# The last attention of four layers recut: scores made turned, their maximum as one more row, and two heads' values side by side

## The reference

```python
def _L3_xattn_ref(x, latents, ...):          # x: context, latents: layer-normed x
    xn = layer_norm(x, ln_media_w, ln_media_b)
    zn = layer_norm(latents, ln_lat_w, ln_lat_b)
    q = (zn @ Wq)                             # 8 heads of 64
    kv_in = jnp.concatenate([xn, zn], axis=1) # 64 + 1024 = 1088 keys
    k, v = kv_in @ Wk, kv_in @ Wv
    sim = jnp.einsum('bhqd,bhfd->bhqf', q * scale, k)   # scale = 1/8
    alphas = jax.nn.softmax(sim, axis=-1)
    out = jnp.einsum('bhqf,bhfd->bhqd', alphas, v)
    return out @ Wout

x = x + jnp.tanh(g_ffn[2]) * _L2_ffn_ref(_layernorm(x, axis=-1), ...)     # quantised
x = x + jnp.tanh(g_xattn[3]) * _L3_xattn_ref(ctx_1024, _layernorm(x, axis=-1), ...)
x = x + jnp.tanh(g_ffn[3]) * _L3_ffn_ref(_layernorm(x, axis=-1), ...)
```

## Time and profile before

| | us |
|---|---|
| median of 3 runs | 2302.47 |
| lowest and highest run | 2296.79, 2312.04 |
| the profiled execution | 2311.39 |
| span of the profiled core, first to last instruction | 2309.5 |
| TensorE busy | 1847.4 (80%) |
| VectorE busy | 1343.0 (58%) |
| ScalarE busy | 1051.7 (46%) |
| GpSimd busy | 570.2 (25%) |
| mean granted clock of TensorE | 0.879 |

### The profile page before, as it was taken

The page is one execution under the profiler, slowest core; times in us unless marked ns, Lnnn a source line. Parts: engine busy times, 40 slices in busy tenths (PEclk is TensorE's granted clock), DMA queues, the critical chain, the costliest instruction groups (busy, mean ns, idle before and its releaser), DMA issues.

```text
span 2309.5 us, 30543 instructions
## 1 busy us (share of the span) xinstructions
PE 1847.4 (80%) x10608; PEld 1326.6 (57%) x10608; DVE 1343.0 (58%) x2559; ACT 1051.7 (46%) x2069; POOL 570.2 (25%) x800
## 2 busy tenths in 40 slices
PE   6643999808975788884998687899999999986895
PEld 3243998805653322253554355688888888873553
DVE  4942444354758466651112688688888888843334
ACT  3112434203226777731221344687876787730340
POOL 2133000072347444432000455101001000105014
PEclk8756999959978699985999887899999999987997
DMA  9112222120000000042112100000000000022343
GB/s 368 45 62 74 105 89 109 36 75 1 1 18 1 1 1 1 1 174 92 32 37 76 37 1 1 1 1 1 1 1 1 1 1 1 1 101 72 99 135 91
DMA packets 60099, 112.53 MB, mean 49 GB/s; under 512 B 7829, under 2 KB 51288, under 8 KB 57520
## 3 DMA queue, kind: packets, MB, share of 16 engines
q1 hardware_dynamic: 52272, 90.02, 11.0%
q0 software_dynamic: 7680, 20.57, 2.8%
HBM read 71.12 MB, written 39.80 MB: 48 GB/s over the span
## 4 chain that ended last, share of the span: by engine, by line
PE 62%; DVE 14%; POOL 8%; ACT 7%; issue 5%; DMA 2%; another core or an unknown queue 1%; SPq 0%; POOLq 0%; DVEq 0%; ACTq 0%
PE psum L203 53%; PE psum L2005 4%; POOL arena L1577 2%; POOL arena L781 2%; ACT arena L1376 2%; POOL xb L776 2%; PE psum L237 1%; DVE arena L518 1%; DVE arena L208 1%; DVE arena L218 1%; POOL arena L678 1%; DVE arena L1458 1%; ACT arena L2067 1%; DVE rounded L2089 1%
## 5 line engine op out<-in xcount | busy, mean ns | idle before, releaser
L203 PE MATMUL psum<-arena 128*128 128x256 f32 (+17 forms) x4423 | 1036.9, 448 | 184.7 <-DVE arena L1492 30.6
L203 PEld LDWEIGHTS psum<-arena 128*128 128x128 f32 (+5 forms) x4423 | 559.6, 177 | 577.7 <-issue 345.1
L203 PE MATMUL psum<-rounded 128*128 128x256 f32 (+5 forms) x3648 | 559.1, 308 | 20.0 <-DVE rounded L817 19.6
L203 PEld LDWEIGHTS psum<-rounded 128*128 128x128 f32 (+2 forms) x3648 | 493.9, 189 | 57.9 <-issue 17.7
L2089 DVE SCALAR_TENSOR_TENSOR rounded<-psum,rounded 128x512 fp32r<-128x512 f32 (+4 forms) x456 | 255.8, 586 | 92.8 <-ACT rounded L2075 43.6
L2075 ACT ACTIVATE rounded<-psum 128x512 fp32r<-128x512 f32 (+1 forms) x320 | 164.6, 553 | 35.8 <-PE psum L2009 18.7
L781 POOL DMA_INDIRECT arena<-yb,arena x80 | 78.0, 974 | 409.2 <-DMA yb<-arena 363.4
L1376 ACT ACTIVATE arena<-psum,arena 128x1024 f32<-128x1024 f32 (+1 forms) x192 | 156.5, 911 | 46.5 <-PE psum L203 46.4
L2115 DVE TENSOR_REDUCE arena<-psum 128x1 f32<-128x1024 f32 x128 | 155.4, 1214 | 1.0 <-PE psum L203 1.0
L2005 PE MATMUL psum<-arena 128*128 128x128 f32 x1024 | 141.3, 278 | 13.2 <-ACT arena L2070 9.3
L2067 ACT ACTIVATE arena<-psum,arena 128x1024 f32<-128x1024 f32 x128 | 143.7, 1123 | 1.7 <-DVE arena L2117 1.7
(11 more groups left out here) (251 smaller groups left out, 2071.3 us busy)
## 6 DMA issues: line engine op xcount, KB each, us to landing
arena<-in_w SPq DMA_DIRECT2D x8, 2048.0 KB, 7.6
yb<-arena SPq DMA_DIRECT2D x102, 128.0 KB
xb<-arena SPq DMA_DIRECT2D x5, 2048.0 KB, 17.3
arena<-xb SPq DMA_DIRECT2D x70, 128.0 KB, 2.2
arena<-in_w1u SPq DMA_DIRECT2D x4, 2048.0 KB, 14.8
arena<-xb SPq DMA_DIRECT2D x8, 512.0 KB
arena<-in_w1d SPq DMA_DIRECT2D x1, 4096.0 KB, 13.5
arena<-in_w3b SPq DMA_DIRECT2D x1, 4096.0 KB, 16.9
```

What stands on the lines that cost most here:

```text
L203: return e.matmul(o, l, r, start=start, stop=stop, skip_group_check=True)
```

## The change

The stage is cut into 16 blocks (G) of one pair of heads and 512 queries; `a` is the head of the pair, j one of nine key tiles (eight of 128 keys, one of the 64 of the context).

- Scores are made turned: keys in PSUM's partitions, 512 queries in its columns. So the exponentials come out as the value matmuls want them, and the transposes, their copies and low parts go. `K1`/`Q1` hold the high part of the head `a`'s k and q in one half of the rows and k's high part (a copy) against q's low part in the other; `K2`/`Q2` hold k's low part against q's high part, and, in rows that were free, ones against the negated maximum. Each score is the sum of two rounded matmuls.
- The maximum now is a rough one, from the high parts alone: an unturned score product of one pass (`pe_rough3`), a maximum on VectorE (`dve_rough3`, `dve_maxima3`), turned on TensorE (the "m" side step) and copied into `Q2` as one more row. It is made for block G + 1 while block G runs.
- Values: v and the exponentials stay unrounded float32. Two matmuls of 64 weight columns, one for each head, write the halves of bank 4's partitions (`pe_values3`).
- The sums over keys: GpSimd adds up the exponentials of the nine tiles (`pool_sum3`), a matmul with ones sums over partitions (the "s" side step), and VectorE takes the reciprocal in four parts and multiplies (`dve_divide3`). The result is already as the output projection ("o") wants it.
- Side steps (q, k, v, m, s, o) come at fixed steps j of a block (`side3`), all in PSUM bank 7 after the first ones.
- The first three side steps are moved into `pe_mid`, `act_mid` and `dve_mid` (rounds 18 to 22); the loads of the next stage's weights come earlier.

```diff
@@ dve_mid, pe_mid, act_mid
+                if 20 <= i < 23 and STAGES >= 7:
+                    dve_side3(e, FIRST3[i - 20])
...
+                if i == 18:
+                    e.wait_ge(s_w3, 16)
+                    e.wait_ge(s_xt, 52)
+                    e.wait_ge(s_scp, NT)
+                if 18 <= i < 21 and STAGES >= 7:
+                    pe_side3(e, FIRST3[i - 18])
...
+                if 18 <= i < 21 and STAGES >= 7:
+                    act_side3(e, FIRST3[i - 18])
@@ the order of the side steps
+        FIRST3 = [("k", 0, 0), ("k", 0, 1), ("q", 0, 0), ("k", 0, 2), ("v", 0, 0), ("v", 0, 1), ("v", 0, 2), ("q", 1, 0),
+                  ("m", 0, 0)]
+        FIRST_BANK3 = (0, 1, 2, 7, 0, 1, 4, 7, 7)
+        def side3(G, j):
+            n = G // 2
+            if j == 1 and G:
+                return ("s", G - 1, 0)
+            if j == 2 and G + 2 < 16:
+                return ("q", G + 2, 0)
+            if 3 <= j <= 5 and n + 1 < 8:
+                return ("v" if G % 2 else "k", n + 1, j - 3)
+            if 6 <= j <= 7 and G >= 7 and (G - 1) // 2 % 4 == 3:
+                return ("o", G - 1, j - 6)
+            if j == 8 and G + 1 < 16:
+                return ("m", G + 1, 0)
+            return None
@@ side steps
+        def pe_side3(e, s):
+            kind, a, c = s
+            bk, was = SIDE3_BANK[s], SIDE3_WAS[s]
+            if was is not None:
+                if was[0] == "o":
+                    e.wait_ge(s_x, 96 + tiles3(was[1], was[2])[1] + 1)
+                elif was[0] in "kq":
+                    e.wait_ge(s_lo3, SIDE3_LOW[was])
+                else:
+                    e.wait_ge(s_mo, SIDE3_KEPT[was])
...
+            if kind == "k":
+                n = 512 if c < 2 else 64
+                for k in range(2):
+                    m = mm(e, psum[:, bk, 0:n], x3_WK[:, k, 128 * p:128 * p + 128], src[:, k, :], k == 0, k == 1)
+            elif kind == "v":
+                for x in range(4 if c < 2 else 1):
+                    for k in range(2):
+                        m = mm(e, psum[0:rows, bk, 128 * x:128 * x + 128], src[:, k, rows * x:rows * x + rows],
+                               x3_WV[:, k, 128 * p:128 * p + 128], k == 0, k == 1)
+            elif kind == "q":
+                b, p, h = block3(a)
+                for k in range(2):
+                    m = mm(e, psum[:, bk, :], x3_WQ[:, k, 128 * p:128 * p + 128],
+                           XT[:, k, 1024 * b + 512 * h:1024 * b + 512 * h + 512], k == 0, k == 1)
+            elif kind == "m":
+                e.wait_ge(s_mx, 48 + a + 1)
+                for t in range(4):
+                    m = mm(e, psum[0:65, bk, 128 * t:128 * t + 128], x3_NM[:, t, :], ident, True, True)
+            elif kind == "s":
+                e.wait_ge(s_pa, 8 * a + 8)
+                for x in range(2):
+                    m = mm(e, psum[64 * x:64 * x + 64, bk, :], ones[:, 0:64], x3_AC[:, a % 2, x, :], True, True)
...
+        def act_side3(e, s):
...
+            if kind == "k":
+                for x in range(2):
+                    src = psum[high3(x), bk, 0:512 if c < 2 else 64]
+                    for r in (high3(x), high3(1 - x)):
+                        e.activation(x3_K1[r, a % 2, x, keys3(c)], src, ACT.Copy).then_inc(s_mo, 1)
...
+            elif kind == "q":
+                for x in range(2):
+                    r = high3(x)
+                    e.activation(x3_Q1[r, a % 3, x, :], psum[r, bk, :], ACT.Copy).then_inc(s_mo, 1)
+                    e.activation(x3_Q2[r, a % 3, x, :], psum[r, bk, :], ACT.Copy).then_inc(s_mo, 1)
+            elif kind == "m":
+                e.activation(x3_Q2[0:64, a % 3, 1, :], psum[0:64, bk, :], ACT.Copy).then_inc(s_mo, 1)
+                e.activation(x3_Q2[64:65, a % 3, 0, :], psum[64:65, bk, :], ACT.Copy).then_inc(s_mo, 1)
...
+        def dve_side3(e, s):
...
+            if kind in "kq":
+                e.wait_ge(s_mo, SIDE3_KEPT[s])
+                for x in range(2):
...
+                    e.scalar_tensor_tensor(out=lo, in0=psum[r, bk, 0:64 if (kind, c) == ("k", 2) else 512], scalar=1.0, in1=hi,
+                                           op0=ALU.mult, op1=ALU.subtract).then_inc(s_lo3, 1)
...
@@ rough scores and maxima
+        def pe_rough3(e, G, i):
...
+            if G:
+                e.wait_ge(s_ar, at)
+            elif at >= 2:
+                e.wait_ge(s_ar, at - 1)
+            if i == 0:
...
+                for t in range(4):
+                    for a in range(2):
+                        m = mm(e, psum[:, bk, 128 * t + 64 * a:128 * t + 64 * a + 64],
+                               x3_Q1[:, G % 3, a, 128 * t:128 * t + 128], x3_K1[:, n % 2, a, 1024:1088], True, True)
+            else:
+                t, a = (i - 1) // 2, (i - 1) % 2
+                for c in range(2):
+                    m = mm(e, psum[:, bk + c, :], x3_Q1[:, G % 3, a, 128 * t:128 * t + 128],
+                           x3_K1[:, n % 2, a, 512 * c:512 * c + 512], True, True)
+            m.then_inc(s_am, 1)
...
+        def dve_maxima3(e, G):
+            e.wait_ge(s_ar, 9 * G + 9)
+            settle(e, dve, e.tensor_reduce(x3_M1, x3_MX, AX.X, ALU.max))
+            for a in range(2):
+                m = e.tensor_scalar(x3_NM[:, :, 64 * (1 - a)], x3_M1[:, :, a], -1.0, None, ALU.mult)
+            m.then_inc(s_mx, 1)
@@ scores, values, exponentials, sums
+        def pe_scores3(e, G, j):
+            n, g, rows = G // 2, 9 * G + j, 128 if j < 8 else 64
+            kt = slice(128 * j, 128 * j + rows)
+            if g >= 2:
+                e.wait_ge(s_ex, 48 + g - 1)
+            for a in range(2):
+                mm(e, psum[0:rows, 2 * (g % 2) + a, :], x3_K1[:, n % 2, a, kt], x3_Q1[:, G % 3, a, :], True, False)
+            if j == 0:
+                e.wait_ge(s_mo, SIDE3_KEPT["m", G, 0])
+            for a in range(2):
+                r = slice(0, 65 if a == 0 else 128)
+                m = mm(e, psum[0:rows, 2 * (g % 2) + a, :], x3_K2[r, n % 2, a, kt], x3_Q2[r, G % 3, a, :], False, True)
+            m.then_inc(s_sc, 1)
+        def pe_values3(e, G, j):
+            n, g, rows = G // 2, 9 * G + j, 128 if j < 8 else 64
+            e.wait_ge(s_ex, 48 + g + 1)
+            if j == 0 and G:
+                e.wait_ge(s_oc, G)
+            for a in range(2):
+                m = mm(e, psum[64 * a:64 * a + 64, 4, :], x3_VF[0:rows, n % 2, j, 64 * a:64 * a + 64], x3_P[0:rows, g % 4, a, :],
+                       j == 0, j == 8)
+            m.then_inc(s_pv, 1)
+        def act_weigh3(e, G, j):
...
+            if g >= 4:
+                e.wait_ge(s_pv, 40 + g - 3)
+                e.wait_ge(s_pa, 8 * ((g - 4) // 9) + max((g - 4) % 9, 1))
...
+            e.activation(x3_P[0:rows, g % 4].rearrange("p a n -> p (a n)"),
+                         psum[0:rows, bk:bk + 2, :].rearrange("p a n -> p (a n)"), ACT.Exp, scale=0.125).then_inc(s_ex, 1)
...
+        def dve_divide3(e, G, i):
...
+            m = e.reciprocal(x3_RC[:, 128 * i:128 * i + 128], x3_SM[:, 128 * i:128 * i + 128])
+            if i == 3:
...
+                e.tensor_tensor(ov, ov, x3_RC, ALU.mult).then_inc(s_on, 1)
+        def pool_sum3(e, G, j):
...
+                m = e.tensor_tensor(ac, ac, x3_P[0:rows, g % 4], ALU.add)
+            m.then_inc(s_pa, 1)
@@ TensorE's order, behind the transposed context, k(0,2), nine rough steps with v and q(1) among them, and m(0)
+            for G in range(16):
+                for j in range(9):
+                    pe_scores3(e, G, j)
+                    if j == 0 and G + 1 < 16:
+                        pe_rough3(e, G + 1, 0)
+                    if j >= 2:
+                        pe_values3(e, G, j - 2)
+                    elif G:
+                        pe_values3(e, G - 1, j + 7)
+                    if j < 8 and G + 1 < 16:
+                        pe_rough3(e, G + 1, j + 1)
+                    if side3(G, j):
+                        pe_side3(e, side3(G, j))
```

More of the change, by code:

```diff
@@ L2148, in steps3 @@
[L2148 to L2158 removed]
+        x3_WO, x3_CN, x3_CT = view(oW + 3072, 4, 256), m_CN, view(oCTX, 2, 128)
+        x3_K1, x3_K2 = rview(o, 2, 2, 1088), rview(oW + 4096, 2, 2, 1088)
+        x3_Q1, x3_Q2 = rview(o + 4352, 3, 2, 512), rview(oAW, 3, 2, 512)
@@ new lines, in build @@
+        SIDE3 = FIRST3 + [side3(G, j) for G in range(16) for j in range(9) if side3(G, j)] + [("s", 15, 0), ("o", 15, 0),
+                                                                                               ("o", 15, 1)]
+        SIDE3_AT = {s: i for i, s in enumerate(SIDE3)}
+        SIDE3_BANK = {s: FIRST_BANK3[i] if i < 9 else 7 for i, s in enumerate(SIDE3)}
+        SIDE3_WAS = {s: next((x for x in SIDE3[:i][::-1] if SIDE3_BANK[x] == SIDE3_BANK[s]), None) for i, s in enumerate(SIDE3)}
@@ new lines, in pe_side3 @@
+        def pe_side3(e, s):
[8 more added lines that the diff above has]
+                    e.wait_ge(s_mo, SIDE3_KEPT[was])
+            if kind in "kv":
```

(28 more changed lines are left out.)

485 lines of the change are left out of this document (141 added, 344 removed).

## The result

| | before | after |
|---|---|---|
| median, us (4 runs each) | 2302.79 | 2333.32 |
| lowest and highest run | 2296.79, 2312.04 | 2330.16, 2335.8 |
| ratio to before, 95% interval | | 1.0121, 1.0096 to 1.0146 |
| span of the profiled execution | 2309.5 | 2331.1 |

The change made the kernel 1.2% slower. The forecast was 4.9% faster, 2190 us in a range of 2150 to 2255. So the direction was wrong too, and 143 us are to be found.

The account below looks back on a forecast made before the run. TensorE was taken as the bound, 22.5 us a block; with waits, 16 blocks came to 446 and the stage to 461 us. Span 2309.5 − 125 + 12 (clock) = 2197, predicted median 2190 us, range 2150 to 2255.

Parts of the forecast that it names:

- unrounded, 512 columns: eight in 3.70, 0.44 each: TensorE price from a run of equal instructions: an unrounded matmul of 512 columns costs 0.44 us at full clock.
- two value matmuls side by side (0.44): In each of a block's nine steps, the two heads' value matmuls run together and cost TensorE 0.44 us.
- The waits: TensorE loses 2.1 us per low-part wait behind q or k, 6.3 in blocks making k, and 1.6 at each border.
- Rival 1: Value pairs run in series at 0.88 us each, 63 us come back, 2253 us; chance 8%.
- Rivals 2 and 3: Stage's clock swings, 0.8 on average, 2238 us, 10%; or stays at half, 2450 us in all, 3%.
- Rival 4: GpSimd's sums become the bound, from 3.3 us a sum; 2200 to 2210 us; chance 6%.
- Rival 5: Side chain binds less, copies and low parts shorter or overlapping: at most 59 us less, 2131; chance 5%.
- pairs a few ns apart: Sign in the profile after: value matmuls of 64 columns start in pairs a few ns apart.
- their group busy below 0.3 us each: Sign in the profile after: the group of 64-column value matmuls is busy below 0.3 us each.
- 75 to 85%: Sign: TensorE's busy share of the stage falls to 75 to 85%, no longer 98%.
- The start: First scores of the last attention stage come at about 1470 us, near 1465 as before.
- the end: Last addition to x comes at 1931 us instead of 2056, 461 us after the first scores.

Follow-up runs that it names:

- early_border: Changed kernel with low parts started behind two ScalarE copies instead of four, and step 0's second score pass issued later: 0.9922 of the kernel before.
- v_full: Changed kernel with each step's two value matmuls over all 128 columns, in series instead of side by side: 1.0367 of the kernel before.
- v_full_rounded: Changed kernel with full-width value matmuls on rounded operands, k's and q's high parts standing in: 1.0077 of the kernel before.
- spread: Changed kernel with the side steps moved apart to other steps of a block, nothing left out: 1.0295 of the kernel before.
- early_border_vfr: early_border with full-width value matmuls on rounded operands, k's and q's high parts standing in: 0.9743 of the kernel before.

## Why the prediction was wrong

**The step that failed** is the first price of the sum, "unrounded, 512 columns: eight in 3.70, 0.44 each". The number is right for what it measures, one record. It was then used as the price of a matmul, "two value matmuls side by side (0.44)"; measured, that term is 1.01. The trace of before had the sign of it: two ways to count, records and code, that I did not lay beside each other. The eight records of the earlier trace rows at 1291.86 are four matmuls of `pe_heads` (two blocks of columns, two halves of the sum), 0.87 us each; the eight transposes just ahead of them (1289.94) are eight records. For rounded matmuls and transposes the two agree, and they were the ones I had counted (512 and 1024).

Its terms, per block, in TensorE's own work:

| term | predicted | measured, with the rows it is from | more, us |
|---|---|---|---|
| nine value pairs | 9 x 0.44 | 9 x 1.01 (1724.44 to 1725.45) | 5.1 |
| k (every other block) | 1.98 | 2 x 1.42 + 0.47 (1714.29 to 1715.71; 1720.25 to 1720.72) | 0.7 |
| v (every other block) | 1.98 | about 2 x 1.8 + 0.6 (16 records of 128 columns from 1655.98 to 1657.79) | 1.1 |
| q, maxima, sums by ones | 0.88 + 0.44 + 0.44 | 1.3 + 0.8 + 1.0 | 1.3 |
| six rounded matmuls, eight steps | 1.54 | 1.61 | 0.6 |

The k and v terms count half, since each is made in every other block. In all 8.8: 22.5 becomes 31.3, and early_border measured 32.4. Of the 1.1 left, the output projections, also unrounded and so doubled, give about 0.4 (the 7 us that I had for all 16 blocks, once more). About 0.5 is in the rounded matmuls behind the long projections of k: four take 1.41 there (1709.75 to 1711.16), against 1.10 elsewhere (1720.72 to 1721.82). By whole steps, a step with k has 5.96 − 1.39 = 4.57 of work, 1.96 more than a quick one and not 1.42, twice in every other block. The little that remains I have not traced.

The rows of that table that are not shown above are these, from the timeline of TensorE in early_border: the turned maxima (0.81 to the next), the sums by ones (1.01), q (1.31), and a part of v (1.81).

```profile
1640.63 1.06 PE L149 MATMUL psum<-arena 128*65 128x128 f32 x8 [0.61 <-DVE arena L2028]
1641.44 1.52 PE L149 MATMUL psum<-rounded 128*128 128x512 f32 x10
...
1647.63 1.08 PE L149 MATMUL psum<-arena 128*64 128x512 f32 x4
1648.64 1.21 PE L149 MATMUL psum<-rounded 128*128 128x512 f32 x4
...
1651.36 1.88 PE L149 MATMUL psum<-arena 128*128 128x512 f32 x4
1652.67 1.49 PE L149 MATMUL psum<-rounded 128*128 128x512 f32 x4
...
1655.98 2.05 PE L149 MATMUL psum<-arena 128*128 128x128 f32 x16
1657.79 1.18 PE L149 MATMUL psum<-rounded 128*128 128x512 f32 x4
```

**The waits** were right in kind, place and count (28 and 15), and too large in size, for the same reason: TensorE's longer work covers more of the chain. I had 2.1 us for each wait of the chain and 1.6 at the border; the rows show 1.1 to 1.4, and 0.83 after 0.17. By the pitch, 35.8 − 32.4 leaves 3.4 a block, against my 6.0 (half of 6.3 + 2.1, 1.6 and half of 0.4). From my mean of a full block, 28.5 (of 30.4 and 26.6), it is + 9.9 of work and − 2.6 of waits to the 35.8 measured.

**Against before**: TensorE's work in the stage is 16 x 32.4 = 518 us instead of nearly all of 590. Gone are 141 us of transposes; new are the rough products and the doubled unrounded ones, and the values, 142.3 before, take 144 x 1.01 = 145. The gain of some 72 us was eaten by the waits, 16 x 3.4 = 54, by the start, 8 later than 1465.6, by the 17 us from the last copy of values to the last addition (2057.4 to 2074.18), in which TensorE has little to do, and by the 11 us by which the first copy of values comes later than one pitch behind the first scores (46.7 − 35.8). 54 + 8 + 17 + 11 − 72 = 18 is, to a microsecond, the lateness of the last additions, 2074.18 against 2055.55. The 32.4 is early_border's; the changed kernel's own busy share gives 32.1 and 3.7 of waits.

**Rival 1** (value pairs in series) was wrong in its mechanism, as v_full shows. Its price of 0.88 a pair was nearer to the 1.01 measured than my 0.44, but by luck: the doubling comes from the two records of each matmul, not from pairs in series. **Rivals 2 and 3** (clock): the changed kernel was granted 1.00 from 1500 to 2000, in spite of its waits of 1.1 to 1.4 us. The rule of the Trainium skill that I had weighed (TensorE: Matmul & The Clock Gate, "A second HAM failure mode: psum-queue depth-cycling") does not describe it. It does describe v_full_rounded (0.92 on average; 0.57 from 1606 to 1608, behind the wait of 1.84 us, and 1.00 again from 1610) and spread (0.94; 0.50 from 1702 to 1710). early_border_vfr was granted 0.98 within its stage. **Rival 4**: GpSimd's sum took 2.37 us, above the 2.1 that I took and below my bound of 3.0; GpSimd is busy for 261 of 500 us and no bound. **Rival 5** (shorter waits) came true in part, and was overrun by the prices.

**Signs named in advance**: "pairs a few ns apart" held, "their group busy below 0.3 us each" held too, 156.0 / 576 = 0.27, and so was no test, for it is per record again. "75 to 85%" busy was wrong (90%), which is the sign that would have told on sight. The start (1473.5 against 1470) held within a few us; the end (2074 against 1931) did not.

## What to carry to other kernels

Before a duration from the trace becomes the price of an instruction that you plan, count its records against the instructions that the code issues in that place: here an unrounded float32 matmul is two records, and a rounded one is one. Price all that is on the bounding engine by the distance between the starts of whole steps in a steady stretch, not by one record. And when a chain over other engines paces some steps, shorten it first (copy once out of PSUM, duplicate from SBUF, let the low part wait for what it needs alone): here that was worth 1.2% of the whole kernel, and replacing the unrounded value matmuls by rounded ones brought 41 us behind it and 10 without it.

## What the runs showed of the hardware

- Two unrounded matmuls of 512 columns, four records, are 1.31 us to the next start over 128 columns and 1.01 as two halves of 64. The six rounded matmuls behind them take 1.61 instead of 1.79. Side by side therefore saves 0.49 us of a step of 3.10; how much of it is the pair's own, these distances don't part.
- GpSimd's addition of two 128x1024 operands takes 2.37 us; a subtraction of the same size on line 1757 of before, whose second operand repeats each value over 64 columns, takes 1.98.
- ScalarE's exponential of 128x1024 without a bias and a sum takes 1.02 us, against 1.12 with both:

```profile
L2055 ACT ACTIVATE arena<-psum 128x1024 f32<-128x1024 f32 x144 | 147.5, 1024 | 157.9 <-PE psum L149 157.1
...
L2085 POOL TENSOR_TENSOR arena<-arena 128x1024 f32<-128x1024 f32 (+1 forms) x112 | 264.9, 2366 | 188.9 <-ACT arena L2055 188.1
```

- VectorE's reciprocal in four parts of 128 is 4 x 0.94 = 3.77 us (3.35 in one of 512), so the four are 0.4 a block dearer. Those of 128 read from SBUF and that of 512 from PSUM, so this isn't shown to be the split alone.
